# Combining the routed results of groups 1 to 3 on GpSimd in place of VectorE, one tile step later

## The reference

```python
for l in range(4):
    x = x + tanh(g_xattn[l]) * xattn_l(layernorm(x), ctx)   # 16 heads in layers 0 to 2, one in layer 3
    y = ffn_l(layernorm(x))        # a router picks 2 of 8 experts per token (1 in layer 3);
    x = x + tanh(g_ffn[l]) * y     # y = sum over the picks k of weight_k * expert_k(token)
                                   # layer 1 adds a bias; layers 0 and 2 add shared experts
```

## Time and profile before

| what | value |
|---|---|
| time, median of 3 runs (lowest, highest) | 727.24 us (726.75, 727.25) |
| span of the profiled execution | 733.4 us |
| TensorE busy | 581.6 us, 79% |
| VectorE busy | 407.1 us, 56% |
| ScalarE busy | 299.0 us, 41% |
| GpSimd busy | 292.8 us, 40% |

### The profile page before, as it was taken

How to read it: one execution, slowest core, us unless ns; L and a number is a source line. 1 busy time by engine, 2 the same in 40 slices (tenths; PEclk the granted TensorE clock), 3 DMA queues, 4 the chain that set the end, 5 groups by cost and what they waited for, 6 DMA issues and landing times.

```text
span 733.4 us, 13284 instructions
## 1 busy us (share of the span) xinstructions
PE 581.6 (79%) x3758; PEld 466.7 (64%) x3758; DVE 407.1 (56%) x1637; ACT 299.0 (41%) x736; POOL 292.8 (40%) x354
## 2 busy tenths in 40 slices
PE   5798768699947898249995899877899998954991
PEld 3466545599915567139992466644699846743991
DVE  3676654488766666302225875524488775553443
ACT  2455533144425644214442554423244335432660
POOL 3112566266620127735452110674066711172541
PEclk9989869899989987559997998757999996555996
DMA  8990011333272001112215000112133140013214
GB/s 273 210 405 2 23 37 41 70 83 88 68 234 111 2 7 39 39 45 63 67 54 155 1 1 0 33 48 66 33 85 92 53 114 1 0 39 75 61 51 122
DMA packets 56182, 54.84 MB, mean 75 GB/s; under 512 B 8200, under 2 KB 50976, under 8 KB 55056
## 3 DMA queue, kind: packets, MB, share of 16 engines
q1 hardware_dynamic: 48272, 39.75, 18.9%
q0 software_dynamic: 7840, 14.25, 6.1%
HBM read 34.99 MB, written 20.86 MB: 76 GB/s over the span
## 4 chain that ended last, share of the span: by engine, by line
PE 60%; DVE 11%; issue 8%; POOL 6%; ACT 5%; DVEq 4%; DMA 4%; SPq 1%; POOLq 0%; ACTq 0%
PE bank L861 17%; PE bank L873 11%; PE bank L698 5%; POOL slots L554 4%; PE bank L685 4%; PE bank L833 4%; PE bank L816 3%; PE bank L818 2%; DVE x L1501 2%; PE bank L849 2%; PE bank L647 2%; ACT pay L953 2%; PE bank L659 2%; DVE stat L1114 1%; PE bank L671 1%
## 5 line engine op out<-in xcount | busy, mean ns | idle before, releaser
L580 POOL DMA_INDIRECT result<-xn,row x133 | 131.0, 985 | 144.5 <-DVE row L1451 134.4
L554 POOL DMA_INDIRECT slots<-pay,pos x112 | 110.7, 989 | 65.9 <-issue 33.1
L517 POOL TENSOR_TENSOR rstd<-spread,minus_half 128x4 f32<-128x4 f32 (+1 forms) x33 | 34.2, 1035 | 212.4 <-DVE spread L1107 181.3
L861 PE MATMUL bank<-xnT,gat 128*128 128x128 f32 x808 | 110.2, 280 | 2.2 <-DVE gat L1460 2.2
L873 PE MATMUL bank<-w,hsh 128*128 (+1 forms) x752 | 107.7, 279 | 1.7 <-DVE hsh L1467 1.1
L861 PEld LDWEIGHTS bank<-xnT,gat 128*128 128x128 f32 x808 | 99.7, 194 | 3.6 <-ACT xnT L1043 2.6
L873 PEld LDWEIGHTS bank<-w,hsh 128*128 128x128 f32 x752 | 96.3, 195 | 2.6 <-issue 2.6
L698 PEld LDWEIGHTS bank<-vblk,probT 128*128 128x128 f32 x384 | 53.3, 210 | 37.7 <-ACT probT L993 25.2
L698 PE MATMUL bank<-vblk,probT 128*128 128x36 f32 x384 | 55.1, 293 | 14.2 <-ACT probT L993 11.4
L1478 DVE COPY xn<-bank 128x128 f32<-128x128 f32 x110 | 31.5, 286 | 51.7 <-PE bank L873 51.7
L1043 ACT COPY xnT<-bank 128x128 f32<-128x128 f32 x133 | 35.4, 268 | 60.2 <-PE bank L849 56.4
(11 more groups left out here) (234 smaller groups left out, 1085.9 us busy)
## 6 DMA issues: line engine op xcount, KB each, us to landing
xg<-slots SPq DMA_DIRECT2D x133, 64.5 KB
w<-in_w SPq DMA_DIRECT2D x4, 2048.0 KB, 11.9
pay<-result SPq DMA_DIRECT2D x21, 256.0 KB, 4.2
w<-in_w SPq DMA_DIRECT2D x1, 2560.0 KB, 19.4
w<-in_w SPq DMA_DIRECT2D x1, 2304.0 KB, 13.8
result<-xn,row POOLq DMA_INDIRECT x133, 2.2
slots<-zeros SPq DMA_DIRECT2D x1, 2064.0 KB, 27.4
slots<-pay,pos POOLq DMA_INDIRECT x112, 2.4
```

Of the source, the lines that this page charges most:

```text
L517: own(pool.tensor_tensor(rstd[:, lo:hi], spread[:, lo:hi], minus_half[:, lo:hi], ALU.pow))
L554: pool.indirect_dma_start(out=(slots1 if l == 1 else slots)[:, :], out_offset=bass.IndirectOffsetOnAxis(ap=pos[:, t, k:k + 1], axis=0), in ...
L580: pool.indirect_dma_start(out=result[:, :], out_offset=bass.IndirectOffsetOnAxis(ap=row[:, s % TURN:s % TURN + 1], axis=0), in_=ysb[:, s % ...
L861: last = pe.matmul(bank[2 + p][:, c * P:(c + 1) * P], weights[:, c * P:(c + 1) * P], xgT[:, p, :], start=True, stop=True)
```

## The change

GpSimd gets a `combine_last` of its own for groups 1 to 3. It multiplies each pick's rows of the group by the weights in place, adds the two, and adds the sum to `x`: four operations over 4x128 elements per partition, five in layer 2, where the bias row comes first. `own` makes GpSimd wait for its own result before it goes on. A new semaphore `p_x` tells VectorE's statistics that `x` of the group is whole, and `wts` tells GpSimd that the weights are there. VectorE keeps group 0, and all groups after layer 3. For groups 1 to 3 the statistics, roots, scalings, transposes and queries of layers 1 to 3 stand one step later than before (`LATER`).

```diff
+        LATER = [0, 1, 1, 1]
...
+            def combine_last(l, g):
+
+                pool.wait_ge(back[g], 16 * sum(TOPK[:l]))
+                pool.wait_ge(Z["wts"], l)
+                ts = slice(g * GT, (g + 1) * GT)
+                xs = x[:, ts]
+                y = [pay[:, k, ts, 0:D] for k in range(2)]
+                for k in range(2):
+                    last = pool.tensor_tensor(y[k], y[k], wts[:, ts, k:k + 1].to_broadcast([P, GT, D]), ALU.mult)
+                own(last)
+                if l == 2:
+                    pool.tensor_tensor(xs, xs, brow[:].unsqueeze(1).to_broadcast([P, GT, D]), ALU.add)
+                own(pool.tensor_tensor(y[0], y[0], y[1], ALU.add))
+                pool.tensor_tensor(xs, xs, y[0], ALU.add).then_inc(Z["p_x"], 1)
...
-                    (at["stats"], GROUPS, root),
+                    (at["combine"] + LATER[l], GROUPS[1:] if l else (), combine_last),
+                    (at["stats"], (0,), root), (at["stats"] + LATER[l], GROUPS[1:], root),
...
-                    (at["scale"], GROUPS, scale_tokens),
-                    (at["tokens"], GROUPS, copy_tokens),
-                    (at["queries"], GROUPS, copy_queries),
+                    (at["scale"], (0,), scale_tokens), (at["scale"] + LATER[l], GROUPS[1:], scale_tokens),
+                    (at["tokens"], (0,), copy_tokens), (at["tokens"] + LATER[l], GROUPS[1:], copy_tokens),
+                    (at["queries"], (0,), copy_queries), (at["queries"] + LATER[l], GROUPS[1:], copy_queries),
...
+                if l and g:
+
+                    dve.wait_ge(Z["p_x"], (l - 1) * (NG - 1) + g)
...
-                    (at["combine"], GROUPS if l else (), combine_last),
-                    (at["stats"], GROUPS, stats),
+                    (at["combine"], (0,) if l else (), combine_last),
+                    (at["stats"], (0,), stats), (at["stats"] + LATER[l], GROUPS[1:], stats),
```

More of the change, by code:

```diff
@@ L223, in flamingo @@
             "c_stat", "c_root", "c_norm", "c_t", "c_T", "c_k", "c_kT", "c_v", "c_blk",
-            "a_stat", "a_root", "r_stat", "r_root", "r_again", "r_spread", "p_self",
+            "a_stat", "a_root", "r_stat", "r_root", "r_again", "r_spread", "p_self", "p_x",
             "a_sc", "a_xt", "a_xT", "a_q", "a_qT",
@@ L239, in flamingo @@
             "m_pad", "m_diag", "m_row", "m_tab",
-            "s_h", "s_gate", "s_act", "s_y", "s_x",
+            "s_h", "s_gate", "s_act", "s_y", "s_x", "wts",
             "bo_rows", "t_x", "t_xT", "t_w", "t_h", "t_pre", "t_hid", "t_y", "t_ysb", "t_id", "t_go"]
@@ L895, in _ @@
                     (at["next_context"] if l < 3 else 0, (0,) if l < 3 else (), next_context),
-                    (at["tokens"], GROUPS, transpose_tokens),
-                    (at["queries"], GROUPS, queries),
+                    (at["tokens"], (0,), transpose_tokens), (at["tokens"] + LATER[l], GROUPS[1:], transpose_tokens),
+                    (at["queries"], (0,), queries), (at["queries"] + LATER[l], GROUPS[1:], queries),
                     (0, three, scores3), (2, three, transpose3), (3, three, values3),
@@ L1348, in weights @@
                     dve.drain()
-                dve.tensor_scalar(wts[:], wts[:], tg[:, 4 + l:5 + l], None, ALU.mult)
+                dve.tensor_scalar(wts[:], wts[:], tg[:, 4 + l:5 + l], None, ALU.mult).then_inc(Z["wts"], 1)
             def tables(l):
```

## The result

The changed kernel takes 745.7 us (median of 4 runs, 737.8 to 747.2) beside 727.0 for the kernel before on the same chip (726.2 to 727.3): ratio 1.0264, 95% interval 1.0216 to 1.0312, slower by 18.7 us. The prediction was 740.1 with a range of 727 to 752.

The account below looks back on a forecast made before the run. The prediction saw no full engine but a chain of waits in the attention of layers 1 to 3; 1.4 + 1.1 + 10.4 = 12.9 us, added to the median 727.24, gave 740.1, range 727 to 752.

Parts of the forecast that it names:

- Sign and range: Whole kernel: slower, chance 0.80, at 740.1 us with a range from 727 to 752.
- case D: Serial chain of combining, statistics and root, GpSimd operations at about 1.0 to 1.45 us: 735 to 745 us; chance 0.62.
- Price: GpSimd's combining: 1.25 us for an operation, 5.25 us a group, 6.5 in layer 2, against 2.35 on VectorE.
- some 5: Layer 3, sign of being right: VectorE's first statistics wait some 5 us for GpSimd's last addition.
- Layer 3: Serial chain makes the first softmax 7.7 us late, group 2's queries 2.7 more: +10.4 us.
- second swap: Layer 3: group 3's scaling also falls behind an exponential; not priced, left in the range.
- Layer 1: Tile step 2 starts 3.1 us late, tile step 4 at 237.1 in place of 235.65: +1.4 us.
- Layer 2: Later root and scaling of group 1 put tile step 5 at 424.5 in place of 423.45: +1.1 us.
- higher: Time above 735 to 745 us if TensorE's granted clock falls while it waits; no size given.
- A: GpSimd is quick, 0.56 us an operation or less, and VectorE's relief counts: faster, about 723 at 0.45; chance 0.12.
- B: GpSimd operations at 0.56 to 0.75 us: layer 3's losses and layers 1 and 2's gains cancel, 726 to 729.5; chance 0.12.
- C: GpSimd held up by VectorE or slowed by repeated weights, 1.6 us an operation and up: 748 to 755; chance 0.14.

Follow-up runs that it names:

- e1: The whole change (GpSimd combining, later step) in layer 3 alone, layers 1 and 2 as in the kernel before; ratio 1.0155 to the kernel before.
- e3: The later step alone in layers 1 to 3, VectorE combining all groups as in the kernel before; 730.4 us, ratio 1.0068 to that kernel.
- e5: The later step in layer 1 alone, VectorE combining everything, all else as in the kernel before; median 719.7 us, ratio 0.9910 to that kernel.
- e8: The later step in layer 2 alone, VectorE combining everything, all else as in the kernel before; ratio 1.0102 to that kernel.
- e6: The whole change (GpSimd combining groups 1 to 3, one step later) in layer 1 alone; ratio 0.9929 to the kernel before.
- e11: The later step in layer 1 for group 1 alone, VectorE combining everything, all else as in the kernel before; ratio 0.9954 to that kernel.
- e2: The whole change in layers 1 and 2, layer 3 as in the kernel before; ratio 1.0085 to that kernel.
- e10: The whole change (GpSimd combining and later step) in layer 2 alone, all else as in the kernel before; ratio 1.0191 to that kernel.
- e7: As e1, with a fifth GpSimd operation of 128x512 for each of the three groups in layer 3; ratio 1.0198 to the kernel before.
- e4: As e1, with GpSimd combining group 3 ahead of group 2's root in layer 3; ratio 1.0140 to the kernel before.
- e0: The kernel before, unchanged, run again; 12 runs between 721.7 and 729.0 us, ratio 0.9986 to itself.

## Why the prediction was right, and where it was not

**Sign and range** held: slower, inside 727 to 752, and in layer 3 by the serial chain of combining, statistics and root, as case D has it. The time lies 5.6 us over the forecast, just above that case's 735 to 745. That it is not further off is in part luck: the terms of layers 1 and 2 were both wrong, and the two errors have opposite signs.

**Price.** 4.65 us a group against 5.25; in layer 3 the statistics that wait, 3.77 and 6.12 us, are the "some 5". I had called the second input the only known difference from L491; its row shows 32 partitions, bf16 and another operation as well, so it is in part luck that the assumed 1.25 us came near. The Trainium skill, "GPSIMD Engine Reference", section 3.1, had given an estimate of 1.27 us (0.20 us of start kept, the rest scaled); the addition of two inputs took 1.268, so the trace agrees for it, while the multiplication by a repeated weight took 1.042.

**Layer 3** (+10.4): right in mechanism, and in size as far as the interval of e1 (7.3 to 15.2) tells. e1 gives 11.3, and the two profiles 11.4 (80.1 against 68.7). Inside it two errors cancel: the cheaper price, and TensorE's late products, for which I carried 5.46 us over from the earlier trace rows and which took 6.61 in after (3.84 in e1). Not all of it is GpSimd's chain: by e3 less e5 and e8 the later step alone costs some 0.56%, 4 us, in layer 3 (an estimate from three ratios), where the sum had 2.7 for the scaling behind the exponential. The "second swap" that I had left in the range, group 3's scaling behind the next exponential, did happen; the earlier trace rows and after don't single out its price.

**Layer 1** (+1.4) is the step that failed in sign. By e6 it gains 5.2 us. I took the delay of tile step 4 for that of the whole stage. It was smaller (0.3 us), and the rest of the stage is shorter with the later step; e5 shows that the step does it alone, and what in it does stays open (e11).

**Layer 2** (+1.1) failed in size: 11 us by e2 less e6 (1.56%), 14 by e10. The step that failed stands in my first paragraph: the change touches "neither matrix work nor its order". TensorE's list does get the transposes and queries of groups 1 to 3 a step later, and I followed the delay through VectorE and ScalarE to tile step 5 and took that for the whole stage. What the runs showed in its place are two idle times of TensorE (GpSimd's price, 3.05 us in after, and the late step itself, 1.82 us in e8) and TensorE at half clock behind them. I had named the fall of the clock as what would make it "higher", without a price. That the clock is what makes 3 us of waiting into 11 or more is shown for e10's execution by its windows; for the medians it is argued from them, since each kernel has one profile and the falls differ: TensorE was busy for 93.8 us of layer 2 in after and 93.7 in e2, where that layer has the same change, against 102.2 in e10.

**The sum.** Layer by layer, alone: -0.7, +1.9 and +1.55, together +2.75%, against +2.64% for the whole. So the effects add up within the noise, and the 6 us that my sum lacks are layers 1 and 2: -5.2 + 13.9 in place of +2.5. My sum was also made on an execution whose layer 3 already took 68.7 us, the longest unchanged one (63.8 to 68.4 in the others).

**The rivals.** A and B: not reached, since an operation costs 1.04 us at least, above the 0.56 and 0.75 up to which they hold; and e5 beside e6 shows no worth of VectorE's relief. C: VectorE's rows over the whole trace are as long as before (`mx` 634 ns, 635 before; statistics 281 in both), and GpSimd's pair of multiplications took 2.04 us both while VectorE waited (215.77) and amid tile steps (231.34). So nothing was held up here. The Trainium skill, "SBUF — State Buffer", "Who interferes with whom", has VectorE instructions with two SBUF inputs contend with GpSimd's reads; these rows don't test that, since the VectorE instructions that ran beside a combining read one of their two tensors from `bank`, which lies in PSUM, or read one tensor only.

## What to carry to other kernels

Ask what stands in the queue of the idle engine that is to take the work: here, in layer 3, each combining stood in a loop with the statistics and the root, so its whole length counted at every link that nothing else hid (two of three in e7's rows), and ordering the queue otherwise brought the softmax 2.0 us forward (e4). When a change moves waits, follow it to the engine with the most work and ask how long that one now idles, to the end of the stage and not to the first steps: in e10's layer 2, 13.0 of the 15.6 us were TensorE's own slower matmuls. And change tables per stage: the same later step gains 0.9% in layer 1 and costs 1.0% in layer 2; e5, which keeps it in layer 1 alone with VectorE combining, beats both kernels.

## What the runs showed of the hardware

In layer 2 an idle time of TensorE of 1.82 us (417.14 in e8) and one of 3.40 us (408.34 in e10) were followed by a granted clock of 0.50 (419 to 425 in e8, 415 to 425 in e10), 1.2 GHz in place of 2.4, and by pairs of matmuls of 1.91 us in place of 1.02. The length of the idle time doesn't decide it. At the same place e0 idled 0.99 us and kept a clock of 1.00, while e11, whose layer 2 is the unchanged one, idled 0.99 us and fell (the third row is of the view by stretches, with PEclk third from the end):

```profile
419.72 0.22 PE L692 MATMUL bank<-bo_rows,onesb 128*128 128x128 bf16 x1 [0.99 <-DVE x L1249]
...
420.26 1.92 PE L707 MATMUL bank<-kblk,qT 128*128 128x512 f32 x2
...
420.00:430.00 10.00, 10.00 (x26) 5.10 (x25) 4.93 (x19) 2.60 (x5) 1.20 (x2) 0.50 0.00 0
```

The Trainium skill, "TensorE: Matmul & The Clock Gate", "HAM oscillation — how this bites in real kernels", tells of a kernel whose matmuls start at half clock again after each wait for a transfer. The traces of e8, e10 and e11 agree, with waits for other engines; e0's doesn't.

Executions of one kernel differ with this clock: of 29 runs of the kernel before, the shortest took 720.4 us at a mean granted clock of 0.865, the longest 733.3 at 0.848, and beside the later kernels its runs reach from 718.8 to 739.0. A single profile is one draw from these.
